# Attention by blocks of 256 queries, with the maxima taken in waves of four heads and the weighing and sums of a unit in one run

## The chip, the core and the metric

The kernel runs on one core of one Trainium2 chip. The metric is the device time of one execution in microseconds, lower is better. The core has a matrix engine (PE, with its weight loads shown apart as PEld), a vector engine (DVE), a scalar engine (ACT), GpSimd (POOL) and a sync engine (SP) whose queue issues the DMAs here.

## What is computed

Eight images of 384 channels and 32 x 32 pixels pass through three stages, each with a residual addition: a group norm with a correlation convolution, attention over the 1024 pixels as tokens, and a feed-forward layer. The change is in the attention alone:

```python
t = t + _L1_attn_ref(_ln_t(t), Wq, Wk, Wv, Wo, bo)
# with x of shape (8, 1024, 384), H = 12 heads of HD = 32, SCALE = HD ** -0.5
q = (x @ Wq.T).reshape(b, n, H, HD).transpose(0, 2, 1, 3)      # k, v likewise
scores = jnp.einsum('bhqd,bhkd->bhqk', q, k) * SCALE
probs = jax.nn.softmax(scores, axis=-1)
out = jnp.einsum('bhqk,bhkd->bhqd', probs, v)
out = out.transpose(0, 2, 1, 3).reshape(b, n, c)
return out @ Wo.T + bo
```

## The kernel before

The three stages run one after another on all engines. In the attention stage each operand of a float32 product is kept as a high and a low float16 part, and q and k of a group of four heads are stacked as three sets of 32 partitions (high, low, high against high, high, low), so that one matmul over 96 partitions gives a float32 score. Partition 96 of the keys holds ones; partition 96 of the queries gets minus the largest score of each query. So the score matmul over 97 partitions gives the shifted score and ACT's exponential needs no per-query bias.

**The order of work.** An image has three groups of four heads and a group has eight units; a unit is 512 queries and two tiles of 128 keys (`w // 4` and `w % 4` in the code). For each unit and each of its four heads, PE fills two score banks of 512 columns (L912), of three, and ACT takes the exponential of each (L1288). The unit before is weighed meanwhile: four matmuls of 32 columns of v beside each other for each key tile (L946), in float32, which the trace shows as two records per matmul. POOL adds the two key tiles of each head (L1445) and, after every second unit, the sums of both units (L1449), and PE adds these over the keys with a matmul against ones into a bank of its own (`sum_up`, L963). Every 512 queries of a group ACT moves the weighted values out (L1296), DVE inverts the sums through two 32 x 32 block transposes (L1105 to L1111) and multiplies (L1116), and ACT and POOL write the two float16 parts (L1302, L1381).

**The maxima** of a group of heads are worked out while the group before it is attended to. Each item is one head, 128 queries and 512 keys: PE writes it to one of two banks (L925) and DVE reduces it (L1090), eight items a unit. After the 16 items of a head DVE combines the two halves (L1096), PE transposes (L931), ACT writes a row of float16 (L1277), and SP issues one DMA per head into partition 96 of that group's queries (L769). PE waits for these rows only at the first unit of the next group.

**Beside this** a unit carries one of the 18 projections of the next image (L874, nine matmuls, or L884, 36 short ones; units 6 to 23) or one of the six output projections of the image before (L897; units 0 to 5), the layer norm of the next image, and SP's copies that stack q and k (`stack`, L760: 24 DMAs, and one for v at L765). Each engine runs the same written-out schedule in order (`schedule`): a prologue, 24 units per image with the image loop over most of them, and an epilogue. An engine that waits holds up all that stands behind it on its queue, SP's included. The bodies of a unit are written by hand for each engine; this is the one of SP before:

```python
            def unit(b, u, qkv=True, maxima=True):
                g, w = u // UNITS, u % UNITS
                if w == 0:
                    load_row(turn_of(b, u), g, HG - 1)
                elif w % 2 == 0 and maxima:
                    load_row(turn_of(b, u), (g + 1) % GROUPS, w // 2 - 1)
```

The feed-forward stage (L1586, L1601) and the convolution stage are not touched.

## Time and profile before

| what | value |
|---|---|
| median of three runs | 3147.1 us (3146.31 to 3152.84) |
| the profiled execution | 3145.05 us, span 3143.1 us |
| granted TensorE clock, mean | 0.947 of full |
| first instruction of the attention stage on SP | 374.35 us |
| first and last score matmul | 511.27 and 2300.42 us |
| store of the last attention image issued | 2327.76 us |
| busy shares | PE 90%, DVE 60%, ACT 49%, POOL 59% |

Times are microseconds from the start of the span. The profiled execution is one run of its own; its 3145.05 us are 2.05 us under the median. A busy matmul engine is not one at its peak, since a matmul's record goes on until its results are out.

### The profile page before, as it was taken

How to read it: one execution, taken by the hardware profiler on the slowest of the kernel's cores; microseconds unless marked ns; L12 is line 12 of the kernel's file. 1: busy time of each engine (PE TensorE's matmuls, PEld its weight loads, DVE VectorE, ACT ScalarE, POOL GpSimd, SP SyncE). 2: the span in 40 equal slices, each digit the busy share in tenths (PEclk: the TensorE clock that was granted, in tenths of full speed). 3: DMA queues.
4: the chain of work that ended last, by engine and by line, in shares of the span. 5: the costliest groups of instructions: out<-in, count | busy, mean ns of one | idle time of the engine just before them, and what ended most of it. 6: DMA issues, size and time to landing. Idle time of an engine off the chain costs nothing. (4 is left out here: it accounts for less than half of the span.)

```text
span 3143.1 us, 52348 instructions
## 1 busy us (share of the span) xinstructions
PE 2819.9 (90%) x16784; PEld 1103.9 (35%) x16784; DVE 1900.0 (60%) x2871; ACT 1548.7 (49%) x2582; POOL 1849.4 (59%) x1407
## 2 busy tenths in 40 slices
PE   4988568999899899898998998999849999999999
PEld 3545231333233333332332332332114444444444
DVE  6766248777677677677677678776634333333332
ACT  3322023556556556556556556555634444444433
POOL 2323114899899899899899899999950111110110
PEclk8989776999999999999999999999989999999999
DMA  3333230021111211211211211112020011010110
GB/s 143 105 119 105 93 103 18 21 55 28 65 52 28 70 47 28 74 43 28 79 38 43 67 36 47 48 28 68 1 101 21 21 41 40 20 40 26 34 40 20
DMA packets 68754, 163.87 MB, mean 52 GB/s; under 512 B 13585, under 2 KB 17614, under 8 KB 67470
## 3 DMA queue, kind: packets, MB, share of 16 engines
q1 hardware_dynamic: 68494, 160.67, 16.0%
q8 instruction: 131, 2.15, 0.3%
q14 instruction: 129, 1.06, 0.1%
HBM read 59.20 MB, written 37.75 MB: 31 GB/s over the span
## 5 line engine op out<-in xcount | busy, mean ns | idle before, releaser
L1090 DVE TENSOR_REDUCE b_mxp<-b_mx 128x1 f32<-128x512 f32 x1536 | 1013.4, 684 | 445.7 <-PE b_mx L925 435.2
L1288 ACT ACTIVATE b_ex<-b_st 128x512 f32<-128x512 f32 x1536 | 828.1, 594 | 551.3 <-PE b_st L912 546.8
L1445 POOL TENSOR_TENSOR b_pair<-b_ex 128x512 f32<-128x512 f32 x768 | 987.0, 1296 | 144.1 <-ACT b_ex L1288 134.8
L925 PE MATMUL b_mx<-b_kst,b_qst 96*128 96x512 f16 x1536 | 561.8, 395 | 89.6 <-DVE b_mxp L1090 73.0
L1449 POOL TENSOR_TENSOR b_pair<-b_pair 128x512 f32<-128x512 f32 x368 | 491.5, 1336 | 28.9
L912 PE MATMUL b_st<-b_qst,b_kst 97*128 97x512 f16 x1536 | 473.5, 387 | 35.1 <-issue 17.7
L1665 DVE TENSOR_TENSOR c_gs<-c_g,c_gs 128x512 f16<-128x512 f32 x192 | 132.8, 692 | 481.9 <-ACT c_gs L1738 481.8
L1586 PE MATMUL c_hid<-c_z,c_wi 128*128 128x512 f16 x1728 | 405.6, 380 | 10.8 <-DVE c_z L1658 10.8
L946 PE MATMUL b_pv<-b_ex,b_v 128*32 128x512 f32 x3072 | 413.4, 611 | 1.0 <-ACT b_ex L1288 1.0
L1601 PE MATMUL c_acc<-c_gs,c_wo 128*128 128x512 f16 x1728 | 404.0, 379 | 0.1
L925 PEld LDWEIGHTS b_mx<-b_kst,b_qst 96*128 96x128 f16 x1536 | 130.0, 97 | 682.4 <-DVE b_mxp L1090 570.5
L1734 ACT ACTIVATE c_g<-c_hid,c_bias 128x512 f32<-128x512 f32 x192 | 131.4, 684 | 363.4 <-PE c_hid L1586 363.2
L1771 POOL TENSOR_TENSOR c_xs<-c_x 128x512 f32<-128x512 f32 x16 | 21.0, 1311 | 479.4 <-DMA c_x<-after_attention 479.4
L1586 PEld LDWEIGHTS c_hid<-c_z,c_wi 128*128 128x128 f16 x1728 | 169.4, 98 | 227.2 <-issue 19.2
L1601 PEld LDWEIGHTS c_acc<-c_gs,c_wo 128*128 128x128 f16 x1728 | 169.0, 98 | 204.2 <-ACT c_gs L1738 0.6
L912 PEld LDWEIGHTS b_st<-b_qst,b_kst 97*128 97x128 f16 x1536 | 149.6, 99 | 200.6 <-ACT b_ex L1288 50.3
L874 PE MATMUL b_pj<-b_z,b_wq 128*128 128x512 f16 x405 | 117.8, 422 | 21.7 <-issue 11.8
L524 POOL TENSOR_TENSOR a_sqs<-a_sq 128x1024 f32<-128x1024 f32 x8 | 18.8, 2355 | 200.3 <-ACT a_sq L502 200.3
L1738 ACT ACTIVATE c_gs<-c_g 128x512 f16<-128x512 f32 x192 | 120.9, 630 | 6.1
L1771 POOL TENSOR_TENSOR c_xs<-c_sq 128x512 f32<-128x512 f32 x16 | 20.3, 1268 | 168.7 <-ACT c_sq L1715 168.7
L1277 ACT ACTIVATE b_mr<-b_mx 8x128 f16<-8x128 f32 x96 | 25.5, 266 | 190.8 <-PE b_mx L931 190.8
L308 PE MATMUL a_conv<-a_fs,a_wm 128*128 128x512 f16 x432 | 117.1, 422 | 0.0
(159 smaller groups left out, 2897.1 us busy)
## 6 DMA issues: line engine op xcount, KB each, us to landing
a_x<-in_x SPq DMA_DIRECT2D x8, 1536.0 KB, 6.5
a_ob<-a_x SPq DMA_DIRECT2D x8, 1536.0 KB, 7.1
after_conv<-a_ob SPq DMA_DIRECT2D x24, 512.0 KB, 2.6
b_xl<-after_conv SPq DMA_DIRECT2D x8, 1536.0 KB, 6.4
b_qst<-b_staged0q SPq DMA_DIRECT2D x192, 64.0 KB, 2.0
b_kst<-b_staged0k SPq DMA_DIRECT2D x192, 64.0 KB, 2.0
b_v<-b_vstaged SPq DMA_DIRECT2D x24, 512.0 KB, 3.0
b_xr<-after_conv SPq DMA_DIRECT2D x8, 1536.0 KB, 6.6
```

Of the source, the lines that this page charges most:

```text
L912: nc.tensor.matmul(st[(SCORES * u + n) % NST][:, :], kst[g][0:MAXROW + 1, s, kt * P:(kt + 1) * P], qst[g][0:MAXROW + 1, s, half * BANK:(ha ...
L925: nc.tensor.matmul(mx[item % 2][:, :], qst[g][0:MAXROW, h, t * P:(t + 1) * P], kst[g][0:MAXROW, h, half * BANK:(half + 1) * BANK], start=T ...
L946: last = nc.tensor.matmul(pv[h * HEAD:(h + 1) * HEAD, :], v[g][:, kt, h * HEAD:(h + 1) * HEAD], ex[u % 2 * HG + h][:, e * BANK:(e + 1) * B ...
L1090: nc.vector.reduce_max(mxp[h % 2][:, t, half:half + 1], mx[item % 2][:, :], AX_X).then_inc(mx_taken, 1)
L1288: nc.scalar.activation(ex[u % 2 * HG + s][:, e * BANK:(e + 1) * BANK], st[(SCORES * u + n) % NST][:, :], ACT.Exp, scale=SCALE).then_inc(ex ...
L1445: nc.gpsimd.tensor_tensor(both[:, :], e[:, 0:BANK], e[:, BANK:NPIX], ALU.add).then_inc(pair_ready, 1)
L1449: nc.gpsimd.tensor_tensor(both[:, :], both[:, :], pair[s][:, :], ALU.add).then_inc(pair_added, 1)
L1586: last = nc.tensor.matmul(hid[m % NH][:, :], wi[a][:, k, m * P:(m + 1) * P], z[p][b][:, k, :], start=n == 0, stop=n == 8)
L1601: last = nc.tensor.matmul(acc[j][:, :], wo[a][:, m, j * P:(j + 1) * P], gs[m % NS][b][:, :], start=m == 0 and n == 0, stop=m == MC - 1 and ...
L1665: nc.vector.tensor_tensor(gs[m % NS][1][:, :], g[m % NG][:, :], gs[m % NS][0][:, :], ALU.subtract).then_inc(glo_ready, 1)
L1734: nc.scalar.activation(g[m % NG][:, :], hid[m % NH][:, :], ACT.Gelu, bias=bias[:, m:m + 1], scale=1.0 / WSCALE).then_inc(gelu_ready, 1)
L1738: nc.scalar.activation(gs[m % NS][0][:, :], g[m % NG][:, :], ACT.Copy).then_inc(ghi_ready, 1)
```

## The change

An image is now 12 blocks of 256 queries of a group, each with two units of four key tiles. A unit still has eight fills of 512 columns, each of two matmuls of 256 columns, and eight exponentials. There are two score banks instead of three. The maxima use the high parts alone: a wave is four matmuls over 32 partitions each, one per head, in the four row quarters of the array, into four banks at once, and DVE reduces all four in one instruction. A block has four waves, issued six waves ahead of the unit that PE is in: two per unit, one after each half. After the fourth wave of a block DVE reduces, transposes (32 x 32 blocks) and negates, without PE or ACT, and SP loads the rows with 16 DMAs of 32 queries by one or three heads each. The fourth head keeps its row at partition 0 under 32 partitions that are otherwise zero, so its score matmul is 128 deep. PE waits for all 16 DMAs of a block at the block's first score matmul. The weighing and the sums of a unit, both halves, stand in one run near the end of the next unit's second half: 16 weighing matmuls and 8 against ones, all of 256 columns. POOL adds once per head and unit, and no longer adds two units together. The sums share a bank with the weighted values. The inversion of the standard deviation goes through transposes like that of the sums. The prologue no longer works out the maxima of a whole group but of the first block and a half.

```diff
-    NST = 3
-    UNITS = 8
+    IU = 24
+    BLOCKS = IU // 2
+    QUERIES = NPIX // 4
+    WAVES = 2 * IU
+    AHEAD = 6
+    FILLS = 2 * HG
+    NST = 2
+    ROWS = 16 * 4 * (P // ROW)
...
+        mx = N.ps("mx", [P, HG, BANK])
         st = [N.ps(f"st{e}", [P, BANK]) for e in range(NST)]
-        mx = [N.ps(f"mx{e}", [P, BANK]) for e in range(2)]
         pj = N.ps("pj", [P, BANK])
         pv = N.ps("pv", [P, BANK])
-        sm = N.ps("sm", [P, BANK])
...
-            def load_row(turn, g, h):
-                sp.wait_ge(row_ready, turn + 1)
-                sp.dma_start(qst[g][MAXROW:MAXROW + 1, h, :], mr[h % 2][:, :]).then_inc(row_loaded[h], 16)
+            def load_rows(b, x):
+                sp.wait_ge(turned, TURN * (BLOCKS * b + x + 1))
+                g, q0 = x // 4, x % 4 * QUERIES
+                for a in range(P // ROW):
+                    for w in range(2):
+                        for h0, h1, at in ((0, HG - 1, HG - 1), (HG - 1, HG, 0)):
+                            q = q0 + w * P + a * ROW
+                            sp.dma_start(qst[g][at * HEAD:at * HEAD + 1, h0:h1, q:q + ROW],
+                                         shift[a * ROW + w * HG + h0:a * ROW + w * HG + h1, :]
+                                         ).then_inc(row_loaded[x % 2], 16)
...
+            def unit(b, u, qkv=True):
+                if u == 2 and not in_prologue(b):
                     stack(b, 2)
+                if u % 2 and has_wave(b, 2 * u - 1):
+                    load_rows(*((b, (u + 1) // 2) if u < IU - 1 else (b + 1, 0)))
                 if u == 12 and qkv:
                     stack(b + 1, 0)
                 if u == 18 and qkv:
...
+            def scores(b, u, e, s):
+                x, kh = u // 2, u % 2
+                g, q0 = x // 4, x % 4 * QUERIES
+                n = HG * e + s
+                depth = P if s == HG - 1 else 3 * HEAD + 1
+                if kh == 0 and n == 0:
+                    pe.wait_ge(row_loaded[x % 2], ROWS * (BLOCKS // 2 * b + x // 2 + 1))
+                wait(pe, exp_ready, FILLS * (IU * b + u) + n + 1 - NST)
+                for j in range(2):
+                    kt = 4 * kh + 2 * e + j
+                    last = nc.tensor.matmul(st[n % NST][:, j * QUERIES:(j + 1) * QUERIES],
+                                            kst[g][0:depth, s, kt * P:(kt + 1) * P],
+                                            qst[g][0:depth, s, q0:q0 + QUERIES],
+                                            start=True, stop=True)
+                last.then_inc(st_ready, 1)
...
+            def wave(b, h):
+                number = WAVES * b + h + AHEAD
+                x, w = (h + AHEAD) // 4, (h + AHEAD) % 4
+                image, x = (b, x) if x < BLOCKS else (b + 1, x - BLOCKS)
+                g, q0, t, half = x // 4, x % 4 * QUERIES, w // 2, w % 2
+                if w == 0 and x % 4 == 0:
+                    pe.wait_ge(stacked[g], STACKED * (image + 1))
+                wait(pe, mx_taken, number)
+                for s in range(HG):
+                    rows = slice(s * HEAD, (s + 1) * HEAD)
+                    last = nc.tensor.matmul(mx[:, s, :], qst[g][rows, s, q0 + t * P:q0 + (t + 1) * P],
+                                            kst[g][rows, s, half * BANK:(half + 1) * BANK],
+                                            start=True, stop=True, tile_position=(s * HEAD, 0))
+                last.then_inc(mx_ready, 1)
...
             def weigh(b, u, e):
-
-                g, w = u // UNITS, u % UNITS
+                x, kh = u // 2, u % 2
-                if e == 0:
-                    pe.wait_ge(exp_ready, SCORES * (unit_no + 1))
-                for h in range(HG):
-                    last = nc.tensor.matmul(pv[h * HEAD:(h + 1) * HEAD, :],
-                                            v[g][:, kt, h * HEAD:(h + 1) * HEAD],
-                                            ex[u % 2 * HG + h][:, e * BANK:(e + 1) * BANK],
-                                            start=kt == 0, stop=kt == TILES - 1,
-                                            tile_position=(0, h * HEAD))
+                g = x // 4
+                pe.wait_ge(exp_ready, FILLS * unit_no + HG * (e + 1))
+                if kh == 0 and e == 0:
+                    wait(pe, pv_moved, BLOCKS * b + x)
+                    if x % 4 == 0:
+                        pe.wait_ge(stacked[g], STACKED * (b + 1))
+                for j in range(2):
+                    kt = 4 * kh + 2 * e + j
+                    for s in range(HG):
+                        last = nc.tensor.matmul(pv[s * HEAD:(s + 1) * HEAD, 0:QUERIES],
+                                                v[g][:, kt, s * HEAD:(s + 1) * HEAD],
+                                                ex[u % 2][e][s][:, j * QUERIES:(j + 1) * QUERIES],
+                                                start=kt == 0, stop=False,
+                                                tile_position=(0, s * HEAD))
                 last.then_inc(pv_ready, 1)
-            def sum_up(b, u):
-
-                w = u % UNITS
-                pe.wait_ge(pair_added, STEPS // 2 * (IU * b + u + 1))
-                for h in range(HG):
-                    last = nc.tensor.matmul(sm[h * HEAD:(h + 1) * HEAD, :], ones[:, :],
-                                            pair[HG + h][:, :], start=w % 4 == 1,
-                                            stop=w % 4 == 3, tile_position=(0, h * HEAD))
+                pe.wait_ge(pair_ready, HG * (unit_no + 1))
+                for s in range(HG):
+                    last = nc.tensor.matmul(pv[s * HEAD:(s + 1) * HEAD, QUERIES:BANK], ones[:, :],
+                                            pair[u % 2][s][:, e * QUERIES:(e + 1) * QUERIES],
+                                            start=False, stop=kh == 1 and e == 1,
+                                            tile_position=(0, s * HEAD))
                 last.then_inc(sum_ready, 1)
...
-                def maximum(s, e):
-                    if maxima:
-                        max_scores(group, image, (g + 1) % GROUPS, 8 * w + 2 * s + e)
-
-
-                scores(b, u, 0)
-                if u >= FIRST and qkv:
-                    project(b + 1, u - FIRST)
-                    project_part(b + 1, u - FIRST, 0, 5)
...
-                if lagging:
-                    weigh(*lag, 0)
...
-                if lagging:
-                    weigh(*lag, 1)
...
-                if lagging and u % 2 == 0:
-                    sum_up(*lag)
...
+                for e in range(2):
+                    scores(b, u, e, 0)
+                    if norm and u in (1, 2) and e == 0:
+                        var(b + 1, u - 1)
+                    if load and u >= IU - 2 and e == 1:
+                        mean(b + 2, u - IU + 2)
+                    scores(b, u, e, 1)
+                    if item == 2:
+                        if e == 0:
+                            if u == FIRST:
+                                pe.wait_ge(exp_ready, FILLS * (IU * b + u) + 1)
+                            begin()
+                        part(2 * e, 4)
+                        scores(b, u, e, 2)
+                        part(2 * e + 1, 4)
+                    elif item == e:
+                        begin()
+                        part(0, 2)
+                        scores(b, u, e, 2)
+                        part(1, 2)
+                    else:
+                        scores(b, u, e, 2)
+                    scores(b, u, e, 3)
+                    if e == 1 and lagging(b, u, 1):
+                        weigh(*before(b, u, 1), 0)
+                        weigh(*before(b, u, 1), 1)
+                    if has_wave(b, 2 * u + e):
+                        wave(b, 2 * u + e)
...
-            def take_max(group, item):
-                dve.wait_ge(mx_ready, ITEMS * group + item + 1)
-                nc.vector.reduce_max(mxp[h % 2][:, t, half:half + 1], mx[item % 2][:, :], AX_X
+            def take_wave(b, h):
+                dve.wait_ge(mx_ready, number + 1)
+                nc.vector.reduce_max(mxp[x % 2][:, w // 2, :, w % 2], mx[:, :, :], AX_X
                                      ).then_inc(mx_taken, 1)
+                if w == 3:
+                    block_no = BLOCKS * b + x
+                    dve.wait_ge(mx_taken, number + 1)
+                    nc.vector.reduce_max(top[:, 0:2 * HG],
+                                         mxp[x % 2][:, :, :, :].rearrange("p t h n -> p (t h) n"), AX_X
+                                         ).then_inc(turned, 1)
+                    dve.wait_ge(turned, TURN * block_no + 1)
+                    nc.vector.transpose(top_turned[:, :], top[:, :]).then_inc(turned, 1)
+                    dve.wait_ge(turned, TURN * block_no + 2)
+                    shifted = BLOCKS // 2 * b + (x - 1) // 2
+                    if not (isinstance(b, int) and b == 0 and x == 0):
+                        dve.wait_ge(row_loaded[(x - 1) % 2], ROWS * (shifted + 1))
+                    nc.vector.tensor_scalar(shift[:, :], top_turned[:, :], -1.0, None, ALU.mult
+                                            ).then_inc(turned, 1)
...
+            def exponential(b, u, e, s):
...
+                if lagging(b, u, 2):
+                    act.wait_ge(pv_ready, 2 * (unit_no - 2) + e + 1)
+                    act.wait_ge(pair_ready, HG * (unit_no - 2) + s + 1)
+                act.wait_ge(st_ready, FILLS * unit_no + n + 1)
+                nc.scalar.activation(ex[u % 2][e][s][:, :], st[n % NST][:, :], ACT.Exp, scale=SCALE
+                                     ).then_inc(exp_ready, 1)
...
+            def add_pair(b, u, s):
+                unit_no = IU * b + u
+                pool.wait_ge(exp_ready, FILLS * unit_no + HG + s + 1)
+                if s == 0 and lagging(b, u, 2):
+                    pool.wait_ge(sum_ready, 2 * (unit_no - 2) + 2)
+                nc.gpsimd.tensor_tensor(pair[u % 2][s][:, :], ex[u % 2][0][s][:, :],
+                                        ex[u % 2][1][s][:, :], ALU.add).then_inc(pair_ready, 1)
...
```

## Rows read from the trace of the kernel before

**Rows 1.** Part 1 of the page: engine, busy time, share of the span, instructions.
```profile
PE 2819.9 (90%) x16784; PEld 1103.9 (35%) x16784; DVE 1900.0 (60%) x2871; ACT 1548.7 (49%) x2582; POOL 1849.4 (59%) x1407
```
**Rows 2.** Windows: start:end, length, busy of each engine, PEclk, DMA share, GB/s.
```profile
600.00:800.00 200.00, 184.07 (x1120) 64.61 (x1118) 151.12 (x235) 119.95 (x220) 186.95 (x147) 0.98 0.14 39
...
2000.00:2200.00 200.00, 192.55 (x1166) 63.27 (x1163) 140.51 (x227) 118.98 (x229) 186.66 (x150) 0.99 0.16 48
```
**Rows 3.** Groups by line and form: count, busy us, mean ns, idle before, releasers.
```profile
L1090 DVE TENSOR_REDUCE b_mxp<-b_mx 128x1 f32<-128x512 f32 x1536 | 1013.4, 684 | 445.7 <-PE b_mx L925 435.2
L1445 POOL TENSOR_TENSOR b_pair<-b_ex 128x512 f32<-128x512 f32 x768 | 987.0, 1296 | 144.1 <-ACT b_ex L1288 134.8 <-issue 8.8
L1288 ACT ACTIVATE b_ex<-b_st 128x512 f32<-128x512 f32 x1536 | 828.1, 594 | 551.3 <-PE b_st L912 546.8 <-POOL b_pair L1445 3.2
...
L1449 POOL TENSOR_TENSOR b_pair<-b_pair 128x512 f32<-128x512 f32 x368 | 491.5, 1336 | 28.9
...
L1096 DVE TENSOR_REDUCE b_nm<-b_mxp 128x8 f32<-128x16 f32 x96 | 16.3, 170 | 17.0 <-issue 10.7
```
**Rows 4.** Timeline of PE, from the first score matmul to the last weighing.
```profile
505.51 1.91 PE L843 MATMUL b_pj<-b_xs,b_mean_w 128*128 128x512 f32 x2
...
511.27 1.06 PE L912 MATMUL b_st<-b_qst,b_kst 97*128 97x512 f16 x2
...
2300.42 0.60 PE L912 MATMUL b_st<-b_qst,b_kst 97*128 97x512 f16 x2
...
2302.07 1.92 PE L946 MATMUL b_pv<-b_ex,b_v 128*32 128x512 f32 x16 [1.04 <-ACT b_ex L1288]
```
**Rows 5.** The chain that ended last: start, length, line, matmuls (feed-forward stage).
```profile
2373.35 1.94 PE c_hid L1586 x9
```
**Rows 6.** Timeline of PE in a unit: start, length, line, form, count, idle before.
```profile
1010.44 1.06 PE L946 MATMUL b_pv<-b_ex,b_v 128*32 128x512 f32 x8
1011.44 0.60 PE L925 MATMUL b_mx<-b_kst,b_qst 96*128 96x512 f16 x2
```
**Rows 7.** Timeline of ACT in the same unit.
```profile
1012.30 1.08 ACT L1288 ACTIVATE b_ex<-b_st 128x512 f32<-128x512 f32 x2 [0.70 <-PE b_st L912]
```
**Rows 8.** Timeline of SP: DMAs of one line in a row, start and total length.
```profile
276.29 8.22 SPq L237 DMA_DIRECT2D a_cs<-a_cs  x12
...
458.06 0.87 SPq L743 DMA_DIRECT2D b_xl<-after_conv  x1
...
869.05 7.56 SPq L760 DMA_DIRECT2D b_kst<-b_staged0k  x12
```
**Rows 9.** L769 alone: issue length in ns, min/median/max, first and last start.
```profile
L769 SPq DMA_DIRECT2D b_qst<-b_mr x96: 623/656/729, 478.1 to 2252.9; - x96
```
**Rows 10.** DMA issues: queue, count, KB each, median us from issue to landing.
```profile
b_qst<-b_staged0q SPq DMA_DIRECT2D x192, 64.0 KB, 2.0
```
**Rows 11.** Timeline of SP in the prologue: a small load from DRAM.
```profile
379.52 0.44 SPq L777 DMA_DIRECT2D b_bo<-in_b_o  x1
```
**Rows 12.** Timeline of PE after an idle stretch, the idle time in brackets.
```profile
443.97 4.02 PE L874 MATMUL b_pj<-b_z,b_wq 128*128 128x512 f16 x9 [5.78 <-ACT b_vstaged L1261]
...
447.78 2.46 PE L874 MATMUL b_sm<-b_z,b_wq 128*128 128x512 f16 x9
```
**Rows 13.** Windows of the first units, columns as in rows 2.
```profile
500.00:510.00 10.00, 7.31 (x12) 1.92 (x12) 7.96 (x13) 0.00 (x0) 0.00 (x0) 0.50 0.00 0
510.00:520.00 10.00, 8.51 (x19) 2.03 (x18) 6.06 (x11) 5.98 (x10) 4.33 (x4) 0.50 0.00 1
520.00:530.00 10.00, 8.96 (x36) 2.33 (x36) 6.34 (x10) 8.35 (x11) 9.69 (x9) 0.82 0.00 0
```
**Rows 14.** Timeline of the epilogue: last sums, a transpose, the last store.
```profile
2307.07 1.06 PE L963 MATMUL b_sm<-b_pair,b_ones 128*32 128x512 f32 x8 [3.08 <-DVE b_pair L1174]
...
2308.21 0.72 DVE L1105 STREAM_TRANSPOSE b_inv<-b_sm 128x512 f32<-128x512 f32 x1 [1.19 <-PE b_sm L963]
...
2327.76 0.40 SPq L802 DMA_DIRECT2D after_attention<-b_xr  x1
```

More of the change, by code:

```diff
@@ L984, in prologue @@
                 for h in range(HALVES):
                     mean(1, h)
-                pe.wait_ge(row_of_ones, 3)
-            def unit(b, u, out_proj=True, norm=True, qkv=True, maxima=True, load=False):
-                g, w = u // UNITS, u % UNITS
-                group = GROUPS * b + g + 1
-                image = b + 1 if g == GROUPS - 1 else b
-                lag = (b, u - 1) if u else (b - 1, IU - 1)
-                lagging = not (isinstance(b, int) and b == 0 and u == 0)
+                wait(pe, *free[id(pv)])
```

473 lines of the change are left out of this document (181 added, 292 removed).

## The prediction

> **What bounds the kernel now.** I read the shares of the page first [rows 1], then the windows of the attention stage [rows 2], the costly groups [rows 3] and the timelines. PE leads with 90%, but in the attention stage PE and POOL are both above 92% busy, DVE near 75% and ACT near 60%, so the stage is several engines tied together rather than one at its peak. It is long: the score matmuls start at 511.27 and the last at 2300.42 [rows 4], and 192 units in 1789 us are 9.32 us a unit, 18.6 us for two. The pure PE stream of a unit is smaller. Nine full-rate matmuls of 512 columns take 1.94 us [rows 5], 0.216 each, and a weighing run of one key tile takes 1.00 us from its start to that of the next matmul [rows 6]. So a unit holds 8 score matmuls (1.73), 8 for the maxima (1.73), nine of a projection (1.94), two weighing runs (2.00) and half a run of sums (0.50): 7.9 of 9.32 us.
>
> **What the change takes away.** DVE reduces 8 x 684 ns = 5.5 us a unit now [rows 3]. Two waves of four banks replace that. A reduction of 2048 values lies between four times 0.53 us, if only the 512 values of each count (684 ns less about 0.15 fixed), and 4 x 0.684 = 2.7; I take 2.3, 4.6 us a unit. POOL loses the second additions, 491.5 us in all [rows 3], and keeps four of 1.3 us, 5.2 us a unit: it is no bound any more. PE gives eight matmuls for two waves. One wave costs 0.22 us if its four matmuls run beside each other and 0.86 if they run in turn. No row shows row quarters. Column strips do run side by side: one float32 matmul over the whole array takes 1.91 us at half clock [rows 4, 13], so some 0.95 at full clock, and four strips together take 1.00 [rows 6]. So I take a value near the low end, 0.45, with something for the change of layout. The weighing and sums of a unit are six sets of 256 columns, half of 1.00 us each less what a single run saves in changes: 2.8 us (between 2.6 and 3.0), against 2.5 before.
>
> **A unit that waits for nothing else.** 16 matmuls of 256 columns (1.73), projection (1.94), weighing and sums (2.8) and one wave (0.45), up to the start of its last wave, are 6.9 us. The two score banks make PE wait for ACT: two exponentials in a row take 1.08 us [rows 7], 0.54 each, and a fill needs the bank of two exponentials earlier. I add 0.7 for the waits in the eight fills (0 to 2): **7.6 us**. ACT has 8 x 0.54 = 4.3 us of exponentials, 0.6 of staging and at most 0.9 of moves, so it has room. If nothing else waited, a block of two units would take 15.2 to 16 us instead of 18.6, and this part of the change is a real gain.
>
> **The step that is added to the path: the rows.** The last wave of block x has number 4x+3, is issued six waves ahead, and so stands at the very end of unit 2x-2, behind the weighing run. The block's scores begin unit 2x. There is only unit 2x-1, 7.6 us of PE's work, between them. In that time must follow, each after the other:
> - the wave's own matmuls, 0.4 us (the record of one is 0.38 to 0.39 long);
> - DVE's reduction, 2.3;
> - the small reduction (170 ns [rows 3]), a transpose of 32 columns and the negation of 32 values; a transpose of 512 columns takes 0.72 [rows 14], so each of the two is between 0.05 and 0.3, and with the waits between them I take 0.6 for all;
> - 16 DMAs issued one after the other by SP. In the copies of 64 KB SP needs 7.56 us for 12, 0.63 each; in those of 6 KB from three partitions to three, 8.22 for 12, 0.69 each [rows 8]; a row alone takes 0.656 [rows 9]. So bytes do not make the time. The row DMAs resemble the 6 KB ones most (few partitions, small): 16 x 0.69 = 11.1 (10.1 at 0.63, 11.7 at the 0.729 maximum). The cheapest small issue is 0.44, for a load from DRAM [rows 11]; at that price it is 7.0;
> - the landing of the last, 2.0 [rows 10] (1.3 to 2.3).
>
> That is 16.4 us, against 7.6 of cover. Before, the same wait cost nothing, since a group's rows were issued units ahead, one DMA per head. So PE stands still for about 8.8 us in every block.
>
> The Trainium skill ("DMA: Bandwidth & Descriptors", section on the anatomy of one DMA) puts a DMA's fixed cost at about 2 us, most of it completion, with some 50 ns of sequencer dispatch; by that price 16 issues would be an estimated 0.8 us and the rows would land in time. The spacing of 0.63 to 0.69 us in rows 8 contradicts it for this queue, and the measurement decides.
>
> **The clock after the wait.** After 5.78 us without a matmul PE starts at half clock, 1.2 GHz: nine matmuls take from 443.97 to 447.78, 0.42 each, and the next nine run near full rate [rows 12]. At the start of the units, where the fills are spaced by waits, the granted clock is 0.50 for the whole of 510 to 520 and 0.82 in the next ten [rows 13]. After an idle stretch of 8.8 us unit 2x will therefore begin at half clock, and its first 4 us of dense work count for 2: 1.9 us more, so unit 2x takes **9.5 us** to its last wave. If the clock never comes back inside it, 13.3 (twice 6.9, with the 0.7 mostly covered); if the clock doesn't fall, 7.6.
>
> **The sum.** A block is 16.4 + 9.5 = 25.9 us. 95 such steps lead from unit 0 to the last block: 2460; the last two units have nothing more to wait for: 15. SP also has the stacking, 25 DMAs x 0.63 = 15.8 us, right behind the rows of a block, in front of the next rows; these are due 9.5 + 3.3 = 12.8 us after the unit's start and SP is free some 1 us later, three times per image: 24 us in all. Together 2499, against 1793 now from the first score matmul to the last weighing: **+706 us**. In the prologue the 64 maxima of a whole group go; the stacks are issued first as now, and the load of the next image at 458.06 [rows 8], its four folds of 1.3 us and two means put unit 0 near 473 instead of 511: -38 (between -20 and -45). In the epilogue the last sums come 3 to 4 us after the last weighing, and the transposes and products have twice the width that they will have [rows 14]: -6. The image's load, store and residual load on SP fall into waits. 3145.05 + 706 - 38 - 6 = 3807 for the profiled execution, 2 us more against the median: **3809 us**.
>
> **Rivals.**
> (a) *The rows are hidden*, not slower but faster: this is the case on the other side. If the 16 issues cost no more than about 2.3 us together (the cover of 7.6 less 0.4 + 2.3 + 0.6 + 2.0), PE never waits and a block is 15.2 us: 96 x 15.2 = 1459, less 1793, less 44: 2769 us. It decides at 0.14 us an issue. By the same page of the Trainium skill it would be this way; the rows give at least 0.44 for a small one. 4%.
> (b) *Small row DMAs are cheap to issue*, 0.44 as in rows 11: the chain falls to 12.3, the idle stretch to 4.7, a block to 21.8, 95 x 4.1 = 390 less: 3420. Against it, all rows of copies within the chip's memory have 0.6 or more. 8%.
> (c) *PE stays at half clock* through unit 2x: 13.3 instead of 9.5, 95 x 3.8 = 361 more: 4170. For it speaks that 510 to 520 stays at 0.50 with PE 85% busy [rows 13]; against it, that the projection is dense, as in rows 12. 12%.
> (d) The score fills become the limit through two banks, and DVE and ACT fall behind beside the waves: 2 us more a block at most, 4000. 6%.
> (e) That the change doesn't do what it says (no wait for the block's rows, or another order) and the time stays near that of now: 1%.
> The forecast has 69%, with a range of its own from 3610 (chain 15.4, unit 8.4) to 4010 (chain 17.4, unit 10.6).
>
> **Numbers.** The range reaches down past part of (b) and up past part of (c): 3520 to 4090. This kernel's measurement can tell about 0.2%. Faster 4%, same 1%, slower 95%.
>
> **What the changed profile would show.** Right: the weight loads of the score matmuls wait for the row DMAs, some 95 times and 8 to 9 us each; SP's row DMAs stand in runs of 16 of 10 to 11 us and start 3 us after the wave; PEclk alternates between halves, a mean in the attention stage of 0.7 to 0.85; POOL below 40% in it; DVE's reduction of 2048 at 2.2 to 2.5 us; the last DMA lands 2 us after its issue. Odd units run 7.6 us and are followed by the gap. Wrong: runs of 16 shorter than 3 us or no wait on DMAs at PE; waits on DVE or ACT as the longest; a unit over 12 us without a gap; or rows issued earlier than the wave at the end of unit 2x-2 allows.

## The result, and the profile after

The changed kernel takes **3758.7 us** (median of four runs, 3752.51 to 3766.55) against 3150.0 before on the same chip: a ratio of 1.193 (95% interval 1.191 to 1.196), slower by 609 us. The prediction was 3809 us with a range of 3520 to 4090, and slower with a chance of 95%. The profiled execution is the one of 3752.51 us, with a span of 3750.6 us and a mean granted clock of 0.862, against 0.947 before.

The page first: part 1, and of part 2 the granted clock. These are the lines that answer to [rows 1].

```profile
PE 2840.0 (76%) x23600; PEld 1384.5 (37%) x23600; DVE 1778.7 (47%) x2072; ACT 1576.4 (42%) x2582; POOL 1371.3 (37%) x1096
...
PEclk8898768888888878888888888888877799999999
```

No engine is near full any more. PE's busy time is almost the same as before (2840.0 against 2819.9 us) in a span that is 607.5 us longer, so the time is idle time, and the clock is down in the whole attention stage. The window below answers to the first of [rows 2]: PE is busy 139 of 200 us where it was 184, and POOL 99 where it was 187.

```profile
1000.00:1200.00 200.00, 139.14 (x1290) 66.14 (x1287) 105.92 (x114) 91.63 (x160) 99.21 (x81) 0.83 0.16 46
```

The costly groups of part 5 that answer to [rows 3], with mean duration, idle time before, and releaser:

```profile
L1350 POOL TENSOR_TENSOR b_pair<-b_ex 128x512 f32<-128x512 f32 x768 | 976.0, 1296 | 1214.4 <-ACT b_ex L1226 1212.9
L1062 DVE TENSOR_REDUCE b_mxp<-b_mx 128x4 f32<-128x2048 f32 x384 | 879.4, 2290 | 1129.2 <-PE b_mx L915 1129.2
L899 PE MATMUL b_st<-b_qst,b_kst 97*128 97x256 f16 (+1 forms) x3072 | 644.0, 319 | 682.0 <-DMA b_qst<-b_shift 596.2
```

POOL and DVE now stand idle for over 1100 us each and wait for ACT and PE. Behind them stands the last line: PE's score matmuls wait 596.2 us for the rows that SP loads. The waits by releaser, with total, number of times and longest, show the wait on its matmuls and on its weight loads:

```profile
PE b_st L899 <- DMA b_qst<-b_shift: 596.2, 93, 10.1
...
PEld b_st L899 <- DMA b_qst<-b_shift: 141.8, 22, 9.7
```

The 22 waits of the weight loads are the same stretches of time as the waits of their matmuls in the same blocks, so the two rows are not added: PE waits 596.2 us, in 93 of the 96 blocks, 6.4 us each. Now one block without stacking, from the timelines of the three engines in the chain. PE, with idle time and releaser in brackets; the waves are L915:

```profile
1220.04 1.03 PE L899 MATMUL b_st<-b_qst,b_kst 97*128 97x256 f16 x4 [6.50 <-DMA b_qst<-b_shift]
...
1228.99 0.39 PE L915 MATMUL b_mx<-b_kst,b_qst 32*128 32x512 f16 x4
...
1234.24 1.07 PE L932 MATMUL b_pv<-b_ex,b_v 128*32 128x256 f32 x16
...
1236.97 0.39 PE L915 MATMUL b_mx<-b_kst,b_qst 32*128 32x512 f16 x4
1243.83 1.03 PE L899 MATMUL b_st<-b_qst,b_kst 97*128 97x256 f16 x4 [6.46 <-DMA b_qst<-b_shift]
```

DVE behind the wave of 1228.99:

```profile
1229.44 2.29 DVE L1062 TENSOR_REDUCE b_mxp<-b_mx 128x4 f32<-128x2048 f32 x1 [2.96 <-PE b_mx L915]
1231.77 0.17 DVE L1067 TENSOR_REDUCE b_top<-b_mxp 128x8 f32<-128x16 f32 x1
1231.97 0.21 DVE L1071 STREAM_TRANSPOSE b_top_turned<-b_top 128x32 f32<-128x32 f32 x1
1232.22 0.18 DVE L1076 TENSOR_SCALAR b_shift<-b_top_turned 128x32 f16<-128x32 f32 x1
```

And SP; between the row DMAs of this block and those of the next stands the stacking of a group, 24 DMAs for q and k and one for v:

```profile
1232.43 10.21 SPq L759 DMA_DIRECT2D b_qst<-b_shift  x16
1242.97 1.80 SPq L745 DMA_DIRECT2D b_qst<-b_staged0q  x3
...
1259.06 0.59 SPq L750 DMA_DIRECT2D b_v<-b_vstaged  x1
1259.79 10.26 SPq L759 DMA_DIRECT2D b_qst<-b_shift  x16
```

The block from 1220.04 to 1243.83 takes 23.8 us. The fourth wave of the next block starts 8.95 after the block's start; DVE is done 3.4 us later; SP issues from 3.4 to 13.7 us after the wave; and the scores begin 1.2 us after the last issue ends: 8.95 + 14.84 = 23.79 us. Of these 14.84 us PE has 8.4 of work (the odd unit) and stands still for 6.5. The clock follows, in the windows of this block (start:end, length, the busy times, PEclk, DMA share, GB/s):

```profile
1220.00:1225.00 5.00, 4.92 (x39) 3.66 (x40) 0.81 (x1) 2.79 (x6) 0.00 (x0) 0.64 0.02 3
1225.00:1229.00 4.00, 4.00 (x71) 2.49 (x69) 1.48 (x1) 2.35 (x6) 3.74 (x4) 1.00 0.00 0
1229.00:1237.00 8.00, 7.73 (x116) 5.10 (x112) 6.06 (x8) 5.34 (x10) 5.55 (x6) 1.00 0.02 3
1237.00:1244.00 7.00, 0.54 (x9) 0.20 (x6) 2.62 (x2) 0.00 (x0) 1.28 (x2) 0.76 0.01 0
```

After the wait PE starts at 1.2 GHz (0.64 is a mixture of both levels), and then runs at 2.4 GHz until it stops again.

**The units.** The table is worked out from the traces: the time in us from the first score matmul of a unit to that of the next, a mean over images 1 to 6, units 0 to 23 of an image, and the image's sum. The experiments below are in it, and are read from it.

```
                  0    1    2    3    4    5    6    7    8    9   10   11   12   13   14   15   16   17   18   19   20   21   22   23    sum
before          9.6  9.2 12.6 11.0 10.8 13.4 14.4  8.4  9.1  8.4  9.1  8.4  9.0  8.4  9.1  8.4  9.2  8.4  9.1  8.4  9.0  9.1  9.6  9.2  231.0
after          12.0 15.2 12.8 14.6 12.3 15.4 10.3 14.8  9.4 14.6  9.4 14.5  9.4 17.9  9.4 14.6  9.4 14.7  9.3 17.8  9.4 15.3 10.7 14.5  307.6
e1_ahead10     10.9 14.6 14.3  8.8 10.7 11.8 10.2  8.1  8.1  8.1  8.0  8.0  8.1  8.1  8.1 12.8  9.6  8.0  8.1  8.3  8.1 12.7 11.0  9.0  233.7
e2_eight_dmas  11.4 14.2 14.7  8.8 11.2 11.6 10.7  8.9  7.8  8.6  7.7  8.5  7.7 13.8  9.6  8.5  7.8  8.5  7.8 13.8  9.3  9.3  8.9  9.0  238.0
e3_warm_pe     11.1 20.3 13.2 14.7 12.0 18.0  8.4 14.7  7.7 14.6  7.7 14.5  7.7 20.3  9.5 14.6  7.7 14.7  7.7 19.7  9.9 15.2 10.0 14.4  308.4
e4_split       10.2 15.0 11.1 15.4 12.3 16.2 11.2 14.9  9.8 14.6  9.5 14.5  9.5 17.7  9.5 14.6  9.4 14.6  9.4 18.0  9.4 14.8 10.4 14.5  306.4
e5_ahead8      10.6 15.0 14.0  8.8 10.2 11.2  9.9 14.0  9.1  8.1  8.0  8.0  8.2  8.1  8.1 17.8  9.6  8.0  8.1  8.3  8.2 17.6 11.1  9.0  249.1
e6_ahead10_8   10.7 15.4 13.5  8.8 10.7 12.0 10.3  8.1  8.1  8.1  8.0  8.0  8.1  8.1  8.1  8.2  8.0  8.0  8.1  8.3  8.1  8.3  8.9  9.0  221.1
e7_split_too    8.5 12.8 10.5 10.4 10.5 12.6 10.6  9.2  7.9  9.2  7.8  9.1  7.9  9.2  7.9  9.2  7.8  9.1  7.9 10.9  7.9 11.1  8.9 10.4  227.1
e8_no_sqrt     10.9 12.5  9.4  8.8  9.8 11.7 10.5  8.1  8.1  8.1  8.0  8.0  8.1  8.1  8.1  8.1  8.0  8.0  8.1  8.3  8.1  8.3  9.0  9.0  213.3
e11_early_move  8.5 14.2 10.5  8.6 10.7 13.3 10.4  8.2  7.9  8.0  7.8  7.8  7.9  7.9  7.9  7.9  7.8  7.8  7.9 10.9  7.9  9.9  8.9  8.9  217.5
```

In the row of after, the wait stands in the odd units: 14.5 where nothing disturbs it, and 17.9 in units 13 and 19, where SP's rows have queued behind a bunch of stacking.

### The profile page after: what moved, and what is told of

Read it like the earlier page. It is cut to its first block and busy times, and to the rows that moved or that the text cites. A ratio compares the mean times of both kernels' runs of the same rounds, so it can differ in the third digit from the quotient of the medians.

```text
span 3750.6 us, 65034 instructions
## 1 busy us (share of the span) xinstructions
PE 2840.0 (76%) x23600; PEld 1384.5 (37%) x23600; DVE 1778.7 (47%) x2072; ACT 1576.4 (42%) x2582; POOL 1371.3 (37%) x1096
## 3 DMA queue, kind: packets, MB, share of 16 engines
q1 hardware_dynamic: 95998, 160.66, 13.7%
## 5 line engine op out<-in xcount | busy, mean ns | idle before, releaser
L1062 DVE TENSOR_REDUCE b_mxp<-b_mx 128x4 f32<-128x2048 f32 x384 | 879.4, 2290 | 1129.2 <-PE b_mx L915 1129.2
L899 PE MATMUL b_st<-b_qst,b_kst 97*128 97x256 f16 (+1 forms) x3072 | 644.0, 319 | 682.0 <-DMA b_qst<-b_shift 596.2
L899 PEld LDWEIGHTS b_st<-b_qst,b_kst 97*128 97x128 f16 (+1 forms) x3072 | 258.9, 108 | 1085.7 <-issue 596.8
L932 PE MATMUL b_pv<-b_ex,b_v 128*32 128x256 f32 x6144 | 430.2, 400 | 0.0
L1516 PEld LDWEIGHTS c_hid<-c_z,c_wi 128*128 128x128 f16 x1728 | 169.5, 98 | 227.8 <-issue 19.5
L932 PEld LDWEIGHTS b_pv<-b_ex,b_v 128*32 128x32 f32 x6144 | 187.0, 114 | 154.9 <-issue 61.2
L940 PE MATMUL b_pv<-b_pair,b_ones 128*32 128x256 f32 x3072 | 243.3, 389 | 0.8 <-POOL b_pair L1350 0.8
L915 PE MATMUL b_mx<-b_kst,b_qst 32*128 32x512 f16 x1536 | 165.5, 421 | 33.9 <-DVE b_mxp L1062 33.8
L883 PE MATMUL b_pj<-b_ao,b_wo 128*128 128x512 f16 x432 | 148.8, 488 | 26.7 <-ACT b_xs L1188 22.2
L859 PE MATMUL b_pj<-b_z,b_wq 128*128 128x512 f16 x405 | 139.8, 445 | 13.8 <-ACT b_vstaged L1211 5.9
L867 PE MATMUL b_pj<-b_wv,b_z 128*128 128x128 f16 x1620 | 136.2, 243 | 0.0
L859 PE MATMUL b_pj<-b_z,b_wk 128*128 128x512 f16 x405 | 135.8, 434 | 0.0
```

What stands on the lines that cost most here:

```text
L859: last = nc.tensor.matmul(bank[:, :], ws[kind][a][:, k, g * P:(g + 1) * P], z[b][:, k, part * BANK:(part + 1) * BANK], start=n == 0, stop= ...
L867: last = nc.tensor.matmul(bank[:, t * P:(t + 1) * P], z[a][:, k, at:at + P], ws[2][b][:, k, g * P:(g + 1) * P], start=n == 0, stop=n == 8)
L883: last = nc.tensor.matmul(pj[:, :], ws[3][a][:, k, j * P:(j + 1) * P], ao[c][:, k, h * BANK:(h + 1) * BANK], start=n == 0, stop=n == 8)
L899: last = nc.tensor.matmul(st[n % NST][:, j * QUERIES:(j + 1) * QUERIES], kst[g][0:depth, s, kt * P:(kt + 1) * P], qst[g][0:depth, s, q0:q0 ...
L915: last = nc.tensor.matmul(mx[:, s, :], qst[g][rows, s, q0 + t * P:q0 + (t + 1) * P], kst[g][rows, s, half * BANK:(half + 1) * BANK], start ...
L932: last = nc.tensor.matmul(pv[s * HEAD:(s + 1) * HEAD, 0:QUERIES], v[g][:, kt, s * HEAD:(s + 1) * HEAD], ex[u % 2][e][s][:, j * QUERIES:(j ...
```

## The experiments

Ten kernels ran in three sets, each against the kernel before on the same chip (medians 3147.67 for the first four, 3148.69 for the next four, 3148.36 for the last two). All are edits of the changed kernel.

### Rows issued a block earlier

```diff
-    AHEAD = 6
+    AHEAD = 10
...
                 load_rows(0, 0)
+                load_rows(0, 1)
...
-                    load_rows(*((b, (u + 1) // 2) if u < IU - 1 else (b + 1, 0)))
+                    load_rows(*((b, (u + 3) // 2) if u < IU - 3 else (b + 1, (u + 3) // 2 - BLOCKS)))
```

> Waves and row DMAs run four waves (two units) earlier, 10 ahead instead of 6; the number of row DMAs and all work of the engines stay. Theory (the chain of 14.9 us from a block's last wave to its landed rows has one unit of 8.0 us to hide in): with three units to hide in, the waits of PE on the row DMAs (738 us in the changed kernel) fall under 60 us, POOL, ACT and PE set a block at 16 to 17.5 us instead of 25.5 on average, and the time falls by 95 x 8 to 9.5 us to 2930 us (2850 to 3020), under the kernel before. Rival 1 (the units themselves are slow: half clock, two score banks, the single weighing run): the wait moves to another place and the time stays over 3500. Rival 2 (SP has too much to issue): 12 x 10.3 + 3 x 16.8 = 174 us per image are under the 192 of its 24 units, so it costs only bunches of some us at the stacks; if SP were the bound the time would be over 3050.

Measured: **3154.3 us** (3149.99 to 3165.12, ten runs), a ratio to before of 1.0025 (1.0012 to 1.0038). 604 of the 609 us are gone, with the same work on every engine: the same waves, the same 16 DMAs per block, only four waves earlier. What PE's score matmuls wait for now, one line's own view of this kernel (L900 is the changed kernel's L899):

```profile
its engine sat idle before it (us, times) until:
  ACT b_ex L1227: 393.8, 793
  issue: 125.4, 349
```

No DMA stands there, where 596.2 us did. So the step of the rows, with one unit of cover, is the cause of the loss. But 192 units of 8.05 us are 1546 us, against 1793 for the same stretch before, and with a prologue and an epilogue that are 21.6 and 2.7 us shorter here than before, the profiled execution would take about 2874, where it took 3160.7. The table says where most of the other 287 us are: units 0 to 6 take 81.3 us instead of 56.4, and units 15, 16, 21 and 22 together 46.1 instead of 32.2. That is 39 us an image. The latter come from the bunches of stacking, but not through PE's wait for rows. There is only one buffer `shift`, from which the rows go. DVE may not write the next block's rows into it before SP's DMAs of the last block have landed, and PE's next wave waits for DVE, as DVE and PE show:

```profile
1391.19 0.18 DVE L1077 TENSOR_SCALAR b_shift<-b_top_turned 128x32 f16<-128x32 f32 x1 [7.11 <-DMA b_qst<-b_shift]
...
1393.65 0.39 PE L916 MATMUL b_mx<-b_kst,b_qst 32*128 32x512 f16 x4 [4.42 <-DVE b_mxp L1063]
```

Units 0 to 6 are taken up below.

### Eight DMAs instead of sixteen

One DMA takes the 128 queries of one head out of four partitions, in place of one of 32 queries for three heads or one.

```diff
-                for a in range(P // ROW):
-                    for w in range(2):
-                        for h0, h1, at in ((0, HG - 1, HG - 1), (HG - 1, HG, 0)):
...
+                for w in range(2):
+                    for h in range(HG):
+                        at = 0 if h == HG - 1 else (HG - 1) * HEAD
+                        q = q0 + w * P
+                        sp.dma_start(qst[g][at:at + 1, h, q:q + P], shift[w * HG + h:P:ROW, :]
+                                     ).then_inc(row_loaded[x % 2], 16)
```

> Six waves ahead as in the change, but each block's rows go with 8 DMAs (one head, 128 queries from four partitions each) instead of 16. Theory (SP's issues, 0.64 us each, are the largest piece of the chain): 8 issues fewer are 5.1 us less in each of 95 blocks, 3759 - 490 = 3270 (3220 to 3330), and PE's wait is 3 us a block where it was 6.5 and more. Rival (landing or DVE sets the chain, or an issue of four source partitions costs twice as much): less than 150 us gained, over 3600.

Measured: **3186.3 us** (3185.76 to 3187.12, four runs), a ratio of 1.0123 (1.0106 to 1.0139), 572 us less than the change. SP's and PE's timelines of this kernel, of one block without stacking:

```profile
1343.96 4.46 SPq L759 DMA_DIRECT2D b_qst<-b_shift  x8
```

```profile
1349.53 0.61 PE L898 MATMUL b_st<-b_qst,b_kst 97*128 97x256 f16 x4 [0.49 <-DMA b_qst<-b_shift]
```

The same bytes in half as many DMAs take 4.46 us instead of 10.2, and PE's wait falls from 6.5 to 0.5 us. Eight fewer would have been 5.5 us at the price of before (8 x 0.69), and 5.75 were saved; 1.6 us more come from the clock, which no longer falls in so short a wait (1.00 in the window of 5 us behind it): units 8, 10 and 12 take 7.7 to 7.8 instead of 9.4. It is the number of issues on SP that costs here, not what they carry. What is left are the bunches (units 13 and 19, 13.8 each).

### PE kept busy while it waits

Before it waits for the rows PE runs 24 matmuls of 512 columns whose results are never used; the real scores overwrite them.

```diff
                 if kh == 0 and n == 0:
+                    wait(pe, exp_ready, FILLS * (IU * b + u) - 1)
+                    for _ in range(24):
+                        nc.tensor.matmul(st[0][:, :], kst[g][0:3 * HEAD, 0, 0:P],
+                                         qst[g][0:3 * HEAD, 0, 0:BANK], start=True, stop=True)
                     pe.wait_ge(row_loaded[x % 2], ROWS * (BLOCKS // 2 * b + x // 2 + 1))
```

> 24 matmuls of 512 columns whose result is overwritten are put ahead of PE's wait for a block's rows, 5.2 us of work at full clock, to keep PE busy in the gap of 6.5 us; nothing else changes. Theory (after the wait PE starts at half clock, which makes the unit behind it 9.0 instead of 8.0 us): the mean granted clock rises from 0.86 to over 0.93 and the time falls by 95 x 0.6 to 1.2 us to 3670 (3640 to 3710). Rival 1 (the even unit is longer for other reasons, such as the order of ACT's work): no change, 3750 to 3770. Rival 2 (the added matmuls delay the last part of the chain): slower, over 3775.

Measured: **3746.2 us** (3738.03 to 3754.46, four runs), a ratio of 1.1892 (1.1871 to 1.1912), only 12 less than the change. The timeline of PE and a window of this kernel:

```profile
1244.86 5.35 PE L897 MATMUL b_st<-b_qst,b_kst 96*128 96x512 f16 x24
1251.30 0.61 PE L903 MATMUL b_st<-b_qst,b_kst 97*128 97x256 f16 x4 [1.08 <-DMA b_qst<-b_shift]
```

```profile
1200.00:1400.00 200.00, 174.74 (x1667) 89.90 (x1667) 101.47 (x105) 84.72 (x160) 90.62 (x77) 0.96 0.09 22
```

In the steady blocks the dummies do what they should: a wait of 1.1 us is left, the clock is 0.96, and even units take 7.7 us instead of 9.4. **The half clock costs 1.7 us a block.** The odd unit is as long as before (14.5), since the rows come when they come. The total hides this gain, because in units 1, 5, 13 and 19 the dummies themselves are in the way (20.3, 18.0, 20.3 and 19.7 us, where the change has 15.2, 15.4, 17.9 and 17.8). Per image that is 12.0 us lost, and the other units gain 11.2. The profiled executions, from which the table is worked out, are 2 us apart (3754.46 and 3752.51); that the medians are 12 apart has no explanation here. The Trainium skill ("TensorE: Matmul & The Clock Gate", section on the oscillation of the clock) describes a loop whose wait for a transfer sends each turn back to the lower clock; the granted clock of 0.64 behind the wait of 6.5 us in the window of the change, and 0.96 here, agree with that.

### The weighing split again

```diff
-                    if e == 1 and lagging(b, u, 1):
-                        weigh(*before(b, u, 1), 0)
-                        weigh(*before(b, u, 1), 1)
+                    if lagging(b, u, 1):
+                        weigh(*before(b, u, 1), e)
```

> The weighing and sums of the unit before stand in two runs, one at the end of each half of the unit, instead of one run in the second half. Theory (the block is set by the row chain plus the even unit, and PE's own work in a unit is the same): the even unit changes by -0.3 to +0.2 us, the time is 3735 to 3780. Rival (the single run of 2.7 us starves ACT of fills, 2.4 us idle per unit, and that is part of the loss): the even unit loses 1 to 2 us, 3570 to 3665.

Measured: **3745.2 us** (3744.64 to 3745.58, four runs), a ratio of 1.1897 (1.1877 to 1.1917), 13 less than the change. The steady units are unchanged (9.4 or 9.5, and 14.6): the single run of weighing and sums costs nothing while the rows set the pace. It has its price only where they don't, as the last experiments show.

### Rows issued half a block earlier

```diff
-    AHEAD = 6
+    AHEAD = 8
...
             def unit(b, u, qkv=True):
+                if u % 2 == 0 and has_wave(b, 2 * u - 1):
+                    load_rows(*((b, (u + 2) // 2) if u < IU - 2 else (b + 1, 0)))
                 if u == 2 and not in_prologue(b):
                     stack(b, 2)
-                if u % 2 and has_wave(b, 2 * u - 1):
-                    load_rows(*((b, (u + 1) // 2) if u < IU - 1 else (b + 1, 0)))
```

> Between the change (6 ahead, one unit of cover) and e1 (10 ahead, three units): 8 waves ahead, 16 DMAs per block as in the change, rows issued before the stacking copies of the same unit. Theory: a chain of 14.9 us against two units of 8.05 = 16.1 us of cover waits for nothing in a steady block, so these run at 16.1 us as in e1; behind each of the three stacking bunches of an image (16.8 us of SP) the rows come 10 us late. Time: e1's 3154 plus 8 x 3 x up to 5 us, 3160 to 3270. Rival (the rows cost something at any distance, for instance through their traffic): steady blocks stay over 17.5 us and the time over 3300.

Measured: **3257.3 us** (3253.28 to 3260.62, four runs), a ratio of 1.0341 (1.0325 to 1.0357). The first score matmul's line waits for rows in this kernel:

```profile
  DMA b_qst<-b_shift: 211.7, 29
```

The chain of 14.85 us fits under two units of 8.05, and the steady units from unit 9 on are those of the experiment with ten waves ahead to 0.1 us. Five of these 29 entries are weight loads whose matmuls stand in the list too. The matmuls alone:

```profile
PE b_st L899 <- DMA b_qst<-b_shift: 183.8, 24, 10.5
```

Four of these 24 are 2 to 3 us long. The others, all but one, stand behind the bunches: units 7, 15 and 21 take 14.0, 17.8 and 17.6 us. Here 1.2 us of slack a block is enough for the chain, but not for 16.7 us of stacking in front of it.

### Both, with and without the split

The first and the second edit together:

> e1 and e2 together: 10 waves ahead and 8 DMAs per block. In e1 units 15, 16, 21 and 22 lose 14 us an image behind the stacking bunches. Theory (SP's bunches): 8 issues fewer per block leave SP free in time, so 14 x 8 = 110 us go from e1's 3154: 3045 (3020 to 3080), 3% under the kernel before. Rival (these units are long because of the next image's loads, means and centring on DVE and ACT): 3130 to 3160.

Measured: **3064.0 us** (3054.24 to 3070.56, five runs), a ratio of 0.9722 (0.9708 to 0.9735): 2.8% faster than the kernel before. Units 15, 16, 21 and 22 are at 8.2, 8.0, 8.3 and 8.9: the bunches are gone too, since 8 issues after 25 still end in time.

The split weighing on top of it:

> e6 with the weighing split into a run at the end of each half of the unit, as in e4. With no wait on rows left, PE's own order sets the unit: ACT stands idle 2.2 to 2.5 us per unit behind the single run. Theory (PE is full: 8.05 us of which about 7.6 are its work, so ACT's idle time costs nothing): within 15 us of e6. Rival (the single run starves ACT and the fills after it start late): 0.4 to 0.8 us less in each of 192 units, 75 to 150 us under e6.

Measured: **3122.0 us** (3115.16 to 3125.66, five runs), 0.9910 (0.9897 to 0.9924), 58 us slower than without it, which neither theory had. Even units gain (7.9 for 8.1) and so do the first of an image, but odd ones rise from 8.1 to 9.2. The timelines of PE, ACT and POOL of this kernel, in one odd unit:

```profile
1017.26 1.07 PE L932 MATMUL b_pv<-b_ex,b_v 128*32 128x256 f32 x16 [1.18 <-ACT b_pvs L1233]
...
1016.62 0.59 ACT L1233 ACTIVATE b_pvs<-b_pv 128x512 f32<-128x512 f32 x1
...
1015.27 0.67 POOL L1313 TENSOR_TENSOR b_ao<-b_pvs,b_ao 128x256 f16<-128x256 f32 x1
```

PE waits for the one bank of weighted values, which ACT moves out only behind four exponentials (from 1014.39 to 1016.6). An earlier move would in its turn have to wait for POOL, which reads until 1015.9 from the buffer that the move writes. In the single run the weighing comes half a unit later, and this wait is covered.

### The square root left out

The fastest so far, with ten waves ahead and eight DMAs, with `ACT.Identity` in place of `ACT.Sqrt` in the attention's layer norm. It leaves out the square root, and with it the loads of ACT's tables.

> e6 without the square root of the variance in the attention's norm: the variance plus epsilon is used in its place (left out of the computation), which takes away two pairs of table loads of 1.28 us each per image. Units 0 to 6 of an image take 27 us more than seven steady ones. Theory (two score banks: any other work of ACT stops PE, one for one): the time falls by 8 x 5.1 = 41 us against e6 (30 to 50). Rival (the units are long through DVE's or POOL's share of the norm): less than 10 us.

Measured: **3014.1 us** (3013.01 to 3022.36, four runs), 0.9581 (0.9566 to 0.9595), 50 us less than with it. Units 1 and 2 fall from 15.4 and 13.5 to 12.5 and 9.4. What stands there with the root, on ACT and on PE, in the kernel with eight DMAs:

```profile
1201.45 1.28 ACT L1187 ACT_TABLE_LOAD   x1
1202.75 0.69 ACT L1187 ACTIVATE b_xs<-b_pj,b_eps 128x512 f32<-128x512 f32 x1
1203.45 1.28 ACT L1225 ACT_TABLE_LOAD   x1
1204.75 1.08 ACT L1225 ACTIVATE b_ex<-b_st 128x512 f32<-128x512 f32 x2
```

```profile
1203.49 1.89 PE L882 MATMUL b_pj<-b_ao,b_wo 128*128 128x512 f16 x4 [2.10 <-ACT b_xs L1187]
```

Between two exponentials ACT is away for 3.3 us, twice per image. Where PE stops meanwhile is not at a score bank, as the theory had it, but at the bank `pj` of the projections: the root reads it, and the output projection (L882) may not write it before. In the kernel with ten waves ahead and eight DMAs this wait is 2.1 us in unit 1 and 1.6 in unit 2, and without the root 0.7 and 0.2; the score matmuls' waits for ACT in both units are 2.8 and 2.1 us. PE then starts at half clock. The windows of unit 2 with the root and without it:

```profile
1166.60:1180.10 13.50, 10.51 (x88) 4.24 (x85) 6.29 (x6) 8.58 (x13) 6.22 (x6) 0.87 0.39 112
...
1141.20:1150.60 9.40, 8.71 (x88) 4.02 (x85) 6.29 (x6) 5.91 (x11) 5.21 (x6) 1.00 0.43 104
```

The four loads are 5.1 us, and 7.8 us an image were gained in the table. This is a third of the 25 us in units 0 to 6; the rest isn't told apart by these runs. The kernel before, with three score banks and the same loads, has 80.9 us in these units, against some 61 for seven of its steady ones, so most of the excess isn't new. What a third score bank would give here was not tried. The Trainium skill ("ScalarE: Activation LUTs", section on what a table load costs) gives about 1283 ns for a load, as here, and a drain of about 1380 ns more; no such drain shows between these lines, where each begins within 0.02 us of the end of the one before.

### The move earlier, with and without the split

```diff
                 exponential(b, u, 0, 1)
+                if u % 2 and lagging(b, u, 3):
+                    move_pv(b, (u - 3) // 2)
...
                 exponential(b, u, 0, 3)
-                if u % 2 and lagging(b, u, 3):
-                    move_pv(b, (u - 3) // 2)
...
-                    if u % 2 == 0 and s == 3 and lagging(b, u, 4):
+                    if u % 2 == 0 and s == 1 and lagging(b, u, 4):
                         attended_low(b, (u - 4) // 2)
```

With the split weighing:

> e7 with two moves: ACT takes the weighted values out after the second exponential of an odd unit instead of after the fourth, and POOL writes the low part before its second pair addition instead of before its fourth, since ACT's move waits for that. Theory (in e7 the first weighing of an odd unit stood 1.2 us before the bank that ACT had not moved out, and that is why the split lost): odd units fall from 9.2 to about 8.0, even ones stay at 7.9, the first units of an image stay as short as in e7 (12.8 and 10.5 where e6 has 15.4 and 13.5); time 3122 - 8 x 12 x 1.1 = 3015 (2985 to 3045), under e6's 3064. Rival (the split itself costs, by changes of the array's layout): over 3080.

Without it:

> e6 with the same two moves and the single weighing run kept. Theory (in e6 the bank is always moved out before the single run late in the unit asks for it): within 10 us of e6's 3064. Rival (the moves help by themselves, by ACT's order): 20 us or more less.

Measured: **3028.1 us** (3025.24 to 3031.76, five runs), 0.9615 (0.9602 to 0.9628), with the split, and 3069.4 (3066.44 to 3073.56, five runs), 0.9752 (0.9738 to 0.9765), without it, which is 5 more than the same kernel without the moves. So the moves alone are worth nothing and the split alone costs 58, while both together gain 36 (0.9615 against 0.9722): odd units go from 9.2 back to 7.9, and every steady unit takes 7.8 or 7.9 us. This is the fastest version that computes the whole reference, 3.85% faster than the kernel before. Its window that answers to [rows 2]:

```profile
1000.00:1200.00 200.00, 183.84 (x1989) 92.06 (x1989) 149.98 (x153) 129.63 (x234) 136.82 (x114) 0.97 0.14 38
```

PE is as busy as before (92%), at nearly the same clock (0.97 against 0.98), but a unit is 7.85 us instead of 8.4 to 9.1, and POOL is at 68% instead of 93%.

## Why the prediction was right

**The cause and its place** were as argued: a new step (a wave, a reduction, a turn and 16 issues) with one unit of cover. The first experiment takes the step off the path and nothing else, and returns 604 of 609 us.

**The terms of the chain**, predicted and measured in the block of 1220 to 1244. From the wave to the negated maxima 3.3 us, measured 3.4 (the reduction 2.29, taken as 2.3; the small operations with their waits 0.7, taken as 0.6). The 16 issues 11.1, measured 10.2. The landing 2.0, measured 1.2 from the end of the last issue, or 1.7 from its start: [rows 10] count from the issue, and I had set them behind its end. The chain 16.4, measured 14.8, which is below the 15.4 at which my own range for it began. The issues and the landing were put too high, the landing even beyond its bound of 1.3 where the sum has it, and the part before them 0.1 too low. PE's idle stretch was put at 8.8 us and is 6.4 on average. The issues lie between the two ends as said: by [rows 8] 0.63 to 0.69 each, measured 0.64 from one to the next. The Trainium skill's page "DMA: Bandwidth & Descriptors" has some 50 ns of dispatch in its anatomy of one DMA (drawn there for GpSimd's path); by that rule rival (a) would have come. The traces disagree for SP: 0.51 us is the shortest of 1536 issues here.

**The even unit** 9.5, measured 8.95 to its last wave. Half clock was put at 1.9 us and costs 1.7; the odd unit was put at 7.6 and takes 8.0 from wave to wave, without a price here, since it stands beside the chain. A wave was taken as 0.45 and takes 0.33 to the next matmul, the run of weighing and sums 2.8 and takes 2.7.

**The step that failed is the sum over irregular blocks.** A steady block takes 24.0 us by the table (23.8 in the one shown) instead of 25.9, which over 95 blocks is 182 us less. I counted collisions with the stacking as 24 us in all, 1 us three times per image. The first and last blocks give the mean: from 476.92 to the last block at 2895.52 are 2418.6 us, 25.46 a block, or 140 us over 95 steady ones. By the table, units 13 and 19 have 3.3 us each too much, some 50 us in all, and units 0 to 5 have 10 per image, some 80, which I had no term for. ACT's table loads are part of these, by the experiment without the root; the rest is not shown. So 116 us too little, and 182 too much. The last two units took 19.5 instead of 15, the prologue gave 34.3 instead of 38 and the epilogue 3.5 instead of 6. Together -182 + 116 + 4.5 + 3.7 + 2.5 = -55, and the profiled execution is 3752.5 against 3807. The number is closer than its terms, since two errors of over 100 us have opposite signs; that part is luck.

**The rivals.** (a), hidden rows: refuted for 16 DMAs, and the experiments show what it takes, since with eight of them and ten waves ahead the kernel is faster than before. The 2769 us of this rival were never near; a unit takes 8.05 or 7.85 us and the first seven of an image more. (b), cheap issues: refuted at 0.64 each, though with another shape they cost 0.56. (c), half clock throughout: refuted, the clock is back within 5 us. (d), two banks: not in the steady units; in the first seven of an image, where the excess stands, no run tells what they cost, and the stop that the root causes is at another bank. (e): refuted, PE waits 596 us for the rows.

**The signs** came nearly as listed: the waits on row DMAs in 93 blocks (6.4 us on average, where 8 to 9 were foretold, and on the matmuls, with only 22 on the weight loads too), the runs of 16 of 10.2 us that start 3.4 us after the wave, a clock of 0.83 in the stage and a reduction of 2.29 us. POOL is busy for 50% of the attention window, where I had said below 40%; 37% is its share of the whole span. That sign was worked out badly, since 5.2 us in a unit of 13 are 40% before its other work is added.

## What to carry to other kernels

The small copies here cost SP's queue 0.56 to 0.69 us each, with little regard to what they carry; before splitting a transfer, multiply its DMAs by such a price and hold the product against the work that covers it. A chain that must fit under a cover was mended here by starting it earlier. A bunch on the same in-order queue needs room of its own, and a single buffer behind the chain passes its delay on to other engines. When the largest wait is gone, run the rest of the change again: the split weighing made 13 us of 3759, then lost 58, and together with the earlier moves gained 36, depending on which wait was left.

## What the runs showed of the hardware that was not expected

- An issue's time on SP depends on its form. In the changed kernel SP's line has issues of 509 to 1038 ns with a median of 675; those of three heads take 0.68 us, those of one 0.51 to 0.52, and 0.64 us lie between two starts on average. With four partitions to one, of one head, 8 take 4.46 us. The line of the changed kernel:

```profile
L759 SPq DMA_DIRECT2D b_qst<-b_shift x1536: 509/675/1038, 460.9 to 2893.9; - x192
```

- A stop of PE of 6.5 us costs 1.7 us of half clock behind it, and 24 matmuls without a use avoid that, if nothing else waits for them.
- One reduction of 2048 values of four banks takes 2.29 us, 0.57 for each bank, where one of 512 took 0.684 [rows 3]. Four matmuls of 512 columns in the four row quarters take 0.33 us until the next matmul starts, where four in turn would take 0.86 (0.216 for one [rows 5]).
